# Adding the gates' bias while VectorE evacuates the bank, with one tanh for both halves

## What is computed

```python
# second layer, h = relu(layernorm(x)), 32 x 256 x 384
feat_out = elu(heads(h))                       # 12 masked attention heads of 32
gate = sigmoid(h @ H_w.T + H_b)                # H_b: one bias per feature
x = x + gate * feat_out + (1.0 - gate) * h
```

## Time and profile before

| | |
|---|---|
| median of 3 runs | 1394.42 us (1394.37 to 1395.95) |
| profiled execution | 1395.05 us, its span 1393.1 us |
| granted TensorE clock, mean over the span | 0.978 |
| PE busy | 1302.0 us, 93% |
| PE weight loads busy | 908.3 us, 65% |
| ACT busy | 1261.6 us, 91% |
| DVE busy | 1221.0 us, 88% |
| POOL busy | 904.1 us, 65% |
| the chain that ended last | PE 48%, issue 15%, ACT 15%, DVE 14%, POOL 3% |

### The profile page before, as it was taken

How to read it: one execution, slowest core, us unless ns; L and a number is a source line. 1 busy time by engine, 2 the same in 40 slices (tenths; PEclk the granted TensorE clock), 3 DMA queues, 4 the chain that set the end, 5 groups by cost and what they waited for, 6 DMA issues and landing times.

```text
span 1393.1 us, 39297 instructions
## 1 busy us (share of the span) xinstructions
PE 1302.0 (93%) x10502; PEld 908.3 (65%) x10502; DVE 1221.0 (88%) x4457; ACT 1261.6 (91%) x3731; POOL 904.1 (65%) x1106
## 2 busy tenths in 40 slices
PE   2889999999999999999999999999999999999974
PEld 1567667766666776666677676767667666666642
DVE  3569999989898998989899898999989899999875
ACT  4469999989999999999999999999999999999975
POOL 3357777657766666777766676766667676567743
PEclk8899999999999999999999999999999999999986
DMA  5000000000000000000000000000000000000000
GB/s 151 13 14 15 26 13 27 27 26 14 26 25 13 25 25 26 14 26 15 23 25 25 15 25 26 12 26 25 25 15 25 25 14 26 25 25 3 13 13 24
DMA packets 29845, 33.28 MB, mean 24 GB/s; under 512 B 10464, under 2 KB 29664, under 8 KB 29664
## 3 DMA queue, kind: packets, MB, share of 16 engines
q1 hardware_dynamic: 29664, 31.62, 7.4%
HBM read 19.03 MB, written 12.58 MB: 23 GB/s over the span
## 4 chain that ended last, share of the span: by engine, by line
PE 48%; issue 15%; ACT 15%; DVE 14%; POOL 3%; DVEq 2%; DMA 1%; ACTq 0%; SPq 0%; POOLq 0%
PE job L501 14%; PE pt L574 10%; PE unit L550 7%; PE job L637 5%; DVE unit L986 4%; ACT p L755 4%; PE job L515 4%; ACT p L712 3%; PE job L489 3%; DVE y L993 3%; PE job L592 2%; ACT o1m L773 1%; ACT c L724 1%; DVE bn L868 1%; POOL xn L1115 1%
## 5 line engine op out<-in xcount | busy, mean ns | idle before, releaser
L755 ACT ACTIVATE p<-y,min 128x256 f32<-128x256 f32 x768 | 394.5, 537 | 10.2 <-DVE min L993 10.1
L986 DVE SCALAR_TENSOR_TENSOR unit<-unit,s,dst 128x256 f32<-128x256 f32 x768 | 336.6, 484 | 37.8 <-ACT p L755 33.6
L574 PE MATMUL pt<-ident,p 128*128 128x128 f32 x2304 | 356.6, 280 | 9.4 <-ACT p L755 5.6
L574 PEld LDWEIGHTS pt<-ident,p 128*128 128x128 f32 x2304 | 266.0, 142 | 84.5 <-issue 45.3
L501 PE MATMUL job<-w,h 128*128 128x384 f16 x1728 | 303.9, 328 | 0.9 <-DVE h L884 0.6
L993 DVE CUSTOM_DVE_ANT_0 y<-unit,mask 128x256 f32<-128x256 f32 x768 | 291.6, 417 | 0.3 <-issue 0.2
L1124 POOL TENSOR_SCALAR p<-p,rec 128x256 f32<-128x256 f32 x384 | 188.3, 506 | 116.1 <-DVE rec L927 111.5
L501 PEld LDWEIGHTS job<-w,h 128*128 128x128 f16 x1728 | 167.2, 98 | 107.9 <-DVE h L884 5.6
L763 ACT ACTIVATE pT<-pt 128x512 f32<-128x512 f32 x384 | 230.2, 621 | 7.4 <-issue 6.6
L712 ACT ACTIVATE p<-y,min 128x256 f32<-128x256 f32 x384 | 191.0, 503 | 37.5 <-PE pt L574 24.6
L515 PE MATMUL job<-h,w 128*128 128x256 f16 x1728 | 216.6, 274 | 1.4 <-DVE h L884 1.4
(11 more groups left out here) (109 smaller groups left out, 2234.0 us busy)
## 6 DMA issues: line engine op xcount, KB each, us to landing
xb<-in_x_dram SPq DMA_DIRECT2D x32, 384.0 KB, 3.3
out_dram<-y SPq DMA_DIRECT2D x32, 384.0 KB, 2.5
pT<-in_w_all_dram SPq DMA_DIRECT2D x4, 576.0 KB, 10.4
adj_raw<-in_adj_dram SPq DMA_DIRECT2D x32, 64.0 KB, 1.9
prod<-in_w_all_dram SPq DMA_DIRECT2D x1, 576.0 KB, 5.0
p<-in_w_all_dram SPq DMA_DIRECT2D x1, 576.0 KB, 11.0
out_row<-in_bf_dram SPq DMA_DIRECT2D x1, 192.0 KB, 4.1
gate_b_row<-in_gate_b_dram SPq DMA_DIRECT2D x1, 192.0 KB, 6.2
```

Of the source, the lines that this page charges most:

```text
L574: last = nc.tensor.transpose(pt_ps[u % 2][:, (2 * hh + kt) * P:(2 * hh + kt + 1) * P], probs[:, u % 3, hh, kt * P:(kt + 1) * P], ident[:])
L755: last = op(p1[:, u % 3, hh, :], y1[:, u % YB, hh, :], ACT.Exp, bias=min1[:, u, hh:hh + 1], scale=-1.0, accum_out=sum1[:, t, h:h + 1])
L986: V.scalar_tensor_tensor(leaky[:, hh * T:(hh + 1) * T], bank[:, hh * T:(hh + 1) * T], s8[par][:, t, h:h + 1], dst5[:, c % 2, hh, :], ALU.a ...
```

## The change

The bias matmul and what prepared its operands go. VectorE evacuates each half of the gates' product with one instruction, product times scale plus bias row, into `gtanh`; ScalarE takes one tanh in place over both halves; POOL's gates wait for that tanh. On VectorE's list the two evacuations stand behind SCORES0 2 and SCORES0 3; ScalarE's list loses `GATE 0` and has `TANH 0` where `GATE 1` was.

```diff
@@ "ACT" order
-        C PT1 8, C EXP1 10, C PT1 9, C EXP1 11, A EXP0 0, B GATE 0, A EXP0 1, C PT1 10, C PT1 11, B GATE 1,
+        C PT1 8, C EXP1 10, C PT1 9, C EXP1 11, A EXP0 0, A EXP0 1, C PT1 10, C PT1 11, B TANH 0,
@@ "DVE" order
-        A SCORES0 2, A SCORES0 3, A NORMP0 1, B SCORE_SUM 0, P LN_T0 0, A NORMP0 2, C PV1 2, B DST_T 0,
+        A SCORES0 2, B GATE 0, A SCORES0 3, B GATE 1, A NORMP0 1, B SCORE_SUM 0, P LN_T0 0, A NORMP0 2, C PV1 2, B DST_T 0,
@@ to_rows (PE)
-                if bias:
-                    mm(bank[:, 0:H], ones_b[:], gate_b3[:], start=True, stop=False)
-                    n = 1
@@ gate_proj (PE)
-                if b.ref == 0 and t == 0:
-                    pe.wait_ge(s_gate_b, 1)
                 bank, made = bank_free(b, "GATE", t)
-                to_rows(bank, h16[1], t, WG, bias=True).then_inc(made, 1)
+                to_rows(bank, h16[1], t, WG).then_inc(made, 1)
@@ ACT
-            def gate_(b, par, t):
-                bank, taken = made(b, "GATE", t)
-                if t == 0 and b.ref >= 1:
-                    act.wait_ge(s_gate, n_gate.after(b.back(1), "GATES"))
-                op(gtanh[:, t, :], bank[:, 0:H], ACT.Tanh, scale=post_g[:]).then_inc(taken, 1)
+            def tanh_gates(b, par, _):
+                for t in range(NT):
+                    _, _, taken, value = job(b, "GATE", t)
+                    act.wait_ge(taken, value)
+                op(gtanh[:], gtanh[:], ACT.Tanh).then_inc(s_gt, 1)
@@ gate_bias (DVE, setup)
-                own(V.tensor_scalar(gate_b_row[:], gate_b_row[:], wscale[:, WG:WG + 1], XS, ALU.mult, ALU.mult))
-                for k in range(3):
-                    own(V.tensor_copy(gate_part[:], gate_b_row[:]))
-                    if k == 0:
-                        own(V.tensor_scalar(gate_b3[:], gate_part[:], ident[:, 0:1], None, ALU.mult))
-                    else:
-                        own(V.scalar_tensor_tensor(gate_b3[:], gate_part[:], ident[:, k:k + 1], gate_b3[:],
-                                                   ALU.mult, ALU.add))
-                    if k < 2:
-                        own(V.tensor_tensor(gate_b_row[:], gate_b_row[:], gate_part[:], ALU.subtract))
-                V.tensor_scalar(post_g[:], post[:, WG:WG + 1], 0.5, None, ALU.mult).then_inc(s_gate_b, 1)
+                own(V.tensor_scalar(gate_b_row[:], gate_b_row[:], 0.5, None, ALU.mult))
+                own(V.tensor_scalar(post_g[:], post[:, WG:WG + 1], 0.5, None, ALU.mult))
@@ DVE
+            def gate_in(b, par, t):
+                bank, taken = made(b, "GATE", t)
+                if t == 0 and b.ref >= 1:
+                    dve.wait_ge(s_gate, n_gate.after(b.back(1), "GATES"))
+                V.scalar_tensor_tensor(gtanh[:, t, :], bank[:, 0:H], post_g[:], gate_b_row[:],
+                                       ALU.mult, ALU.add).then_inc(taken, 1)
@@ POOL
-            G.memset(ones_b[:], 1.0)
@@ gates (POOL): waits
-                for (_, _, taken, _), value in zip(jobs_, tanh):
-                    pool.wait_ge(taken, value)
+                pool.wait_ge(s_gt, tanh)
```

More of the change, by code:

```diff
@@ L265, in build @@
         ndT = [sb(f"ndT{i}", [P, T], BF16) for i in range(2)]
-        ones_b = sb("ones_b", [P, P], BF16)
-        gate_b3 = sb("gate_b3", [P, H], BF16)
-        gate_part = sb("gate_part", [P, H], BF16)
         gtanh = sb("gtanh", [P, NT, H])
@@ L338, in build @@
         s_nd, n_nd = sem("s_dst_middle_part"), Count(NB, "DVE", {"SCORE_SUM": 1})
-        s_gate_b = sem("s_gate_bias_parts")
         s_hskip, n_hskip = sem("s_skip_h"), Count(NB, "DVE", {"SKIP_H": 1})
+        s_gt, n_gt = sem("s_gates_tanh"), Count(NB, "ACT", {"TANH": 1})
         s_gate, n_gate = sem("s_gates"), Count(NB, "POOL", {"GATES": 1})
@@ L491, in transpose_norm, with to_rows @@
                 return last
-            def to_rows(bank, rows, t, w, bias=False):
+            def to_rows(bank, rows, t, w):
                 n = 0
-                if bias:
-                    mm(bank[:, 0:H], ones_b[:], gate_b3[:], start=True, stop=False)
-                    n = 1
                 for c in range(NC):
@@ L501, in to_rows @@
                         last = mm(bank[:, 0:H], rows[:, i, c, t * P:(t + 1) * P], w16[:, w, j, c, :],
-                                  start=n == 0, stop=(c, i, j) == (NC - 1, *TERMS[-1]))
+                                  start=n == 0, stop=n == 3 * NC - 1)
                         n += 1
@@ L775, in _ @@
             walk(act, ORDERS["ACT"], {"LN_T0": ln_t0, "Q": q, "V": v, "EXP0": exp0, "PT0": pt0, "PV0": pv0, "LN_T1": ln_t1,
-                       "HEADS": heads, "GATE": gate_, "SCALED": scaled, "EXP1": exp1, "PT1": pt1,
+                       "HEADS": heads, "TANH": tanh_gates, "SCALED": scaled, "EXP1": exp1, "PT1": pt1,
                        "ELU_RELU": elu_relu, "ELU_EXP": elu_exp})
@@ L1029, in _ @@
                        "SCORE_SUM": score_sum, "DST_T": dst_t, "SCORES1": leaky1,
-                       "PV1": pv1, "RECIP1": recip1, "OUT_T": out_t, "FINISH": finish, "SKIP_H": skip_h})
+                       "PV1": pv1, "RECIP1": recip1, "OUT_T": out_t, "FINISH": finish, "SKIP_H": skip_h, "GATE": gate_in})
         @block.gpsimd
@@ L1154, in gates @@
             def gates(b, par, _):
-                jobs_ = [job(b, "GATE", t) for t in range(NT)]
-                tanh = [ready(pool, value) for _, _, _, value in jobs_]
+                tanh = ready(pool, n_gt.after(b, "TANH"))
                 used = ready(pool, n_fin.after(b.back(2), "FINISH", 1)) if b.ref >= 2 else None
                 pool.wait_ge(s_pool_const, 8)
-                for (_, _, taken, _), value in zip(jobs_, tanh):
-                    pool.wait_ge(taken, value)
+                pool.wait_ge(s_gt, tanh)
                 if b.ref >= 2:
```

## The result

The change makes the kernel slower: **1436.24 us** median of 4 runs (1435.94 to 1436.91), against 1394.87 us of the kernel before on the same chip. The ratio is 1.0296, with a 95% interval of 1.0278 to 1.0314. I had forecast 1424 with a range of 1404 to 1432: the sign and most of the steps are right, the time lies 4 us above the range.

A forecast was written before the change was run, and what follows sets the result against it. VectorE (DVE) was taken to close every iteration. 30 x 1.09 us, plus 1.0 for the first and last, minus 4.1 in setup, gave +29.6 us: 1424, range 1404 to 1432.

The forecast's parts named there:

- Part 1: Bias matmul gone from PE: 0.16 us each in the queue, two per iteration, 0.32 us.
- part 3: Who waits behind VectorE's second evacuation: PE stands some 1 us before DST_T; cost 1.09 us per full iteration.
- Part 2: Two evacuations on VectorE: 0.53 us each, 0.36 us wait for GATE 1, NORMP0 1 late by 1.26 us.
- DVE closes every iteration: Reading that VectorE ends each iteration, through layernorm statistics or last SCORES1 units, so its delay counts: 1.09 us each.
- Part 4: One longer tanh on ScalarE for two: LN_T0's high part about 0.5 us later, costed at nothing beside DVE's delay.
- Part 5: Setup: most of the bias's preparation leaves VectorE, 4.1 us come off the path; bounds zero to 4.1.
- A second round trip: Rival: VectorE waits again at SCORES0 4 or DST_T's copy, 0.4 us more per iteration; 1436; chance 0.07.
- Partly hidden: Rival: VectorE has unprinted slack in the first two thirds; about 0.5 us per iteration, +11 (1406); chance 0.14.
- The relieved engines set the pace: Rival, faster: PE and ACT set iteration length, DVE's 0.90 us goes into its idle 12%; 1380; chance 0.09.

The follow-up runs named there:

- WARM: Added step: nine matmuls on PE ahead of QK 0 after each loop jump, into GATE 0's free bank; on the changed kernel 1418.85 us, on the kernel before 1393.07.
- e2: Kernel before plus nine matmuls on PE ahead of QK 0 after the loop's jump, as control; 1393.07 us, ratio 0.9993.
- e3: Kernel before without the two bias matmuls (output not the right one), setup unchanged; 1389.6 us, ratio 0.9970.
- e4: Kernel before plus two idle 128x384 VectorE instructions where the change has its evacuations, result unused; 1425.12 us, ratio 1.0228.
- e5: Kernel before plus the two idle VectorE instructions and the nine matmuls after the jump; 1415.05 us, ratio 1.0144.
- e11: Changed kernel with the nine matmuls, and NORMP0 1 alone moved ahead of GATE 1's evacuation; 1409.31 us, ratio 1.0116.
- e6: Changed kernel with the nine matmuls, GATE 0's evacuation ahead of SCORES0 2, NORMP0 1 ahead of GATE 1's, tanh behind PT0 0; 1407.29 us, ratio 1.0091.
- e1: Changed kernel plus nine matmuls on PE ahead of QK 0 after the loop's jump; 1418.85 us, ratio 1.0181.
- e9: Changed kernel with the nine matmuls, and the tanh alone moved behind PT0 0 on ScalarE; 1418.76 us, ratio 1.0180.
- e10: Changed kernel with the nine matmuls, and GATE 0's evacuation alone moved ahead of SCORES0 2; 1418.85 us, ratio 1.0180.
- e7: Changed kernel with the nine matmuls, plus one overwritten 128x384 matmul ahead of each gate product in the bias matmul's place; 1430.06 us, ratio 1.0249.
- e8: Kernel before with the nine matmuls and the bias preparation moved into VectorE's waits ahead of PV0 1 and LN_T1; 1389.06 us, ratio 0.9963.
- e12: Kernel before with the nine matmuls, late bias preparation, and POOL's mask step behind NORMP0 2; 1387.67 us, ratio 0.9963.

## Why the forecast was right, and where it was wrong

**One rule fits ten kernels.** Between jumps, an interval's change is PE's new wait before DST_T less what PE was relieved of (0.32 us where both bias matmuls are gone):

| | PE's wait | relief | difference | interval, against 40.05 or, with WARM, e2's 40.02 |
|---|---|---|---|---|
| e3 | 0 | 0.32 | −0.32 | −0.33 |
| e4, e5 | 0.48, 0.49 | 0 | +0.48, +0.49 | +0.34, +0.41 |
| e11 | 0.66 | 0.32 | +0.34 | +0.44 |
| e6 | 0.66 | 0.32 | +0.34 | +0.43 |
| changed, e1, e9, e10 | 1.04 | 0.32 | +0.72 | +0.81, +0.82, +0.81, +0.80 |
| e7 | 1.05 | 0 | +1.05 | +1.14 |

The rule holds within 0.14 us. It is bookkeeping on PE, which has hardly another wait between jumps (0 to 0.2 us in all), so by itself it shows no cause. The cause rests on the runs that changed one thing: e3, where the whole of PE's relief shortened these iterations, and e11, where SCORE_SUM came 0.38 us earlier and they were 0.38 shorter. By these, PE, not VectorE, closes the iterations without a jump, and VectorE's delay counts as far as it makes PE stand.

**Part 1** (bias matmul 0.16 us in the queue, 0.32 per iteration) is right: e3 gave 0.33 back, e7 cost 0.32 and 0.35. What it did with that number was wrong; see part 3.

**Part 2** (two evacuations at 0.53, a wait of 0.36 before the second, NORMP0 1 late by 1.26) is nearly right. Timeline of VectorE in the changed kernel:

```profile
671.34 0.61 DVE L930 SCALAR_TENSOR_TENSOR gtanh<-job,post_g,gate_b_row 128x384 f32<-128x384 f32 x1
671.87 0.42 DVE L903 CUSTOM_DVE_ANT_0 y<-unit,mask 128x256 f32<-128x256 f32 x1
...
672.91 0.62 DVE L930 SCALAR_TENSOR_TENSOR gtanh<-job,post_g,gate_b_row 128x384 f32<-128x384 f32 x1 [0.27 <-PE job L495]
673.45 0.15 DVE L910 RECIPROCAL rec<-sum 128x2 f32<-128x2 f32 x1
...
675.61 0.69 DVE L867 SCALAR_TENSOR_TENSOR h<-job,h 128x512 f16<-128x512 f32 x1
676.22 0.15 DVE L910 RECIPROCAL rec<-sum 128x2 f32<-128x2 f32 x1
```

The evacuation is 0.53 us from start to start (671.34 to 671.87) and the wait 0.27. From QK 0's start (666.62 here, 693.86 before) NORMP0 1 comes 6.83 us later instead of 5.68: late by 1.15.

**Part 3 is the step that was wrong in its reading.** PE stands before DST_T for 1.04 us, where I expected some 1 us. But I charged 1.09 us to every iteration because "DVE closes every iteration". PE had its 0.32 us of relief to set against the wait, so iterations without a jump cost 0.81. Those with a jump cost 1.04, and there my term fits. VectorE also had a little room that its waits don't print: NORMP0 2, the second reciprocal of the rows above, starts 0.61 us after LN_T0's low part (675.61 to 676.22), while in the earlier trace rows LN_T0 starts at 701.73 and the corresponding row of the kernel before is

```profile
702.55 0.17 DVE L927 RECIPROCAL rec<-sum 128x2 f32<-128x2 f32 x1
```

0.82 us later. The 0.2 us were waiting for ACT's sum: no bracket shows them here, and e12's does, where they have grown to 0.28. By themselves these errors make the forecast too high: corrected, part 3 is 12 × 1.04 + 19 × 0.86 = 28.8, against my 33.7.

**Part 4** (the tanh costs nothing) is right. ACT waits 18.6 us before it in total, 0.6 each, and moving it away changed nothing (e9). **Part 5** (setup −4.1) is right: 3.7 in the changed kernel, 4.0 alone in e8. The busy times I forecast were not: VectorE's rose by 21.8 us where I had +35, and ScalarE's fell by 6.7 where I had 10. For VectorE I had added rows of 0.61 us that overlap; at 0.53 us it would be +30, and the rest of the difference isn't explained.

**The missing term** is what put the time outside the range. The sum put TensorE's clock at nothing and gave no reason for it: 10 more drops at 1.65 us are +16.5 us. Without them the same steps give 28.8 − 3.7 = +25, which e1 against e2 measured as 25.8, and the forecast of +29.6 would have been 3.8 us off. The bracket of 2.01 us before QK 0 stood in the kernel before, one jump in twelve already had the drop; the mean clock of 0.978 was no sign of it, since the clock is 1.00 from 160 to 1330 us there and lower at the start and the end alone. I read the stall as VectorE's jump and didn't ask what PE's clock does behind it. The mean interval, forecast to go from 40.8 to 41.9 us, went to 42.3.

**The rivals.** *A second round trip* named 1436 and its number was hit by chance, for its mechanism isn't there: VectorE's waits for QK are still two per iteration (48 in 24), and nothing but L930 was added. *Partly hidden* was right in kind for iterations without a jump (0.81 instead of 1.09). *The relieved engines set the pace*: half of it is true, PE does close the iterations without a jump, and e3 shows its 0.32 us; but its condition, 0.9 us of true waiting on VectorE, isn't met. The rule of the Trainium skill (Perfetto Trace Analysis, Identifying the Most-Contended Engine) that pointed to ACT isn't borne out here: ACT's busy time fell by 6.7 us and the time rose, though VectorE had more to do at the same time, and freeing ACT's list at that place gave nothing (e9). With three engines near 90% that hand work to each other several times per iteration, the busy shares didn't tell which of them the time would follow.

**What stays open.** Why the clock falls behind gaps of 1.9 to 2.2 us in 11 of 12 trips of the changed kernel and behind such gaps in one of 12 before. The falls keep a time of their own, and the number of drops differed from kernel to kernel (1, 4, 8, 11) with the trip's length, but no run varied that length by itself. Each number is counted in one execution, and it may differ from one to the next: the runs of the kernel before lie between 1392.2 and 1398.2 us. Open too is why an interval with a jump costs 1.04 to 1.13 us, which no experiment takes apart.

## What to carry to other kernels

An operation moved to an engine that is busy 88% is not hidden in the missing 12%: find the instruction at which another engine would stand for it, and set the relief of that engine against the wait; here 1.04 less 0.32 us, in the iterations that this engine closes. Where a loop's jump or any stall leaves TensorE idle, look at the granted clock behind it in every trip, before and after, since a change that only shifts the trip can bring or remove a drop that is as large as the change itself. A gain found beside the idea (here the setup, 4 us) is often to be had without it.

## What the runs showed of the hardware that I had not expected

- TensorE fell to its lower clock behind gaps of 1.9 to 2.2 us in 11 of 12 trips and behind gaps of the same length in one of 12. In one trip the next two products took 2.08 and 2.31 us instead of 1.13 and 1.63, in another 1.14 and 3.06; the falls were 85.33 us apart whatever the trip did. Nine matmuls of 1.63 us together in the gap kept the clock at 1.00 (e1).
- A VectorE cast of 24 columns took 0.18 us, or 0.48 while POOL made its mask, with its end 0.03 us behind POOL's.
- VectorE loses 2.5 to 3.1 us at the loop's jump in each trip, here 12 times in 33.9 us, and that stall is what opens PE's gap.
